# Graph layer kernel: edge codes spread by broadcasting DMA reads, weighted destination one-hots made by GpSimd alone

## The chip, the cores and the metric

The kernel runs on one core of a Trainium2 chip. The time is the device time of one execution in microseconds (us). The engines are named as the profile names them: PE is TensorE (matmuls), PEld its weight loads, DVE is VectorE, ACT is ScalarE, POOL is GpSimd, SP is SyncE, which here only issues DMAs (SPq is its queue). Each runs its own list of instructions in order; between engines the order is held by semaphores (`wait_ge` and `then_inc`).

## What is computed

```python
# x: 1250 x 512; src, dst: 41250 edges, sorted by dst before the kernel sees them
h = relu(layernorm(x))
m = relu(concat(h[src], h[dst]) @ W0.T + b0)           # one message per edge
x = x + segment_sum(m, src)                            # "S" in the kernel
h = relu(layernorm(x))
g = (h @ W1.T)[src] * edge_weight
out = segment_sum(g, dst)
x = x + where(out >= 0, out, alpha * out)
```

The kernel splits the first product in two (A = h Wa for sources, B = h Wb + b for destinations), so a message is relu(A[src] + B[dst]). The second layer becomes a matrix: M[src, dst] is the sum of the weights of the edges from src to dst, and the result is M.T (h W1.T).

## The kernel before

Nodes stand in 10 blocks of 125. Stage one (to about 339 us) sorts the edges into tiles of 128 that have one source block and one destination block each, puts for each tile the local source number (`local_s`), the local destination number (`local_d`) and the weight (as a high and a low part, `weight_h`, `weight_l`) of each edge on the partitions, and computes A and B, each as a high and a low part. Stage two is the edge loop (to about 1053 us), which the change is in. Stage three is the second layer (to the end).

The edge loop goes over 108 groups (`NGRP`) of 4 tiles (`GRP`); the tiles of a group make two pairs (`PAIR`), called h = 0 and h = 1 here. For group g:

- ACT needs the codes of the edges along the free dimension and on all 125 partitions. `row_d` and `row_s` hold them as one row for each group. PE spreads a row over the partitions by a matmul with a column of the identity (`spread`, L881, into the PSUM tile `spread_ps`), ACT squares the difference to the partition's own number (`square_of`, L990) and turns it into a one-hot (`one_hot_of`, L995: `turned_d`, `turned_s`).
- PE makes a message tile j by four matmuls (L931, L932 with `turned_d`; L936, L937 with `turned_s`) into `edge_ps[j]`. ACT takes the relu and its high part (`msg_hi`, L1014), DVE the low part (`msg_lo`, L1086). PE sums the messages over the sources with two matmuls (`sum_tile`, L886, with the one-hot `hot_s`), DVE adds them to S (`add_sums`, L1059).
- For M, DVE makes one-hots of the destinations (`make_hots(hot_d, ...)`, L1097) and POOL multiplies them with the two parts of the weights (`weigh`, L838, into `hot_w[h]`). PE multiplies them with the one-hots of the sources (`weights`, L896, two matmuls into `m_ps`). ACT copies the result out (`copy_weights`, L1000, into `pair_w[h]`), DVE adds the parts (`join_weights`, L1069), and POOL adds the two 125 x 125 squares to M (`add_weights`, L850). I write W(g, h) for the two matmuls of `weights(g, ..., h)`.

The order around the change is written out by hand:

- PE in group g (L919): tile 0, spread of the destinations of g + 1, sums of tile 2 of g - 1; tile 1, spread of the sources of g + 1, sums of tile 3 of g - 1, W(g - 1, 0); tile 2, sums of tile 0; tile 3, then (L914) sums of tile 1 and W(g - 1, 1).
- DVE in group g (L1081): msg_lo of tile 0; of tile 1, S of g - 1, join of (g - 2, 1); msg_lo of tile 2, `hot_d` of g + 1; msg_lo of tile 3, `hot_s` of g + 1 (L1103, after W(g - 1, 1)), S of g, join of (g - 1, 0).
- POOL in group g (L864): weigh (g, 0), add (g - 1, 0), weigh (g, 1), add (g - 1, 1). `weigh` waits for the matmuls that last read the buffer (L844), `add_weights` for the join (L853). One buffer `hot_w[h]` stands for each h.
- PE waits in `weights(g, ..., h)` for both parts of `hot_w[h]` of g:

```python
pe.wait_ge(hots_w, g * 4 + 2 * h + 2)
```

Of the kernel before, what the change touches and what calls it, by code (L numbers as in the profile page):

```python
# [20 lines left out]
ALU = mybir.AluOpType  # L21
# [9 lines left out]
P = 128  # L31
# [9 lines left out]
GRP = 4  # L41
PAIR = 2
# [34 lines left out]
def build(nc, x, src, dst, edge_weight, w0, b0, w1, alpha, out):  # L77
    table_dram = nc.dram_tensor("edge_table", [P * NT, TABLE_FIELDS], F32).ap()
    with ExitStack() as top:
# [25 lines left out]
        expand_at = sb("expand_at", [1, NGRP, 2 * GRP], I32)  # L105
        gather_at = sb("gather_at", [1, NGRP, 2 * GRP], I32)

# [31 lines left out]
        with ExitStack() as scope:  # L139
            def sb1(name, shape, dt, where=scope):  # L140
                return sb(name, shape, dt, where)


# [115 lines left out]
            with nc.Block() as block:  # L259
# [28 lines left out]
                def _(pool):  # L288
# [70 lines left out]
                    own(pool.tensor_copy(weight_h[:], weight_all))  # L359
                    pool.tensor_tensor(weight_l[:], weight_all, weight_h[:].bitcast(F32), ALU.subtract)  # L360

                @block.vector
                def _(dve):
# [191 lines left out]
                    own(dve.tensor_scalar(local_d[:], code[:].bitcast(I32), 1.0 / 65536.0, None, ALU.mult))  # L555
                    own(dve.tensor_scalar(local_s[:], local_d[:], -(TILE - 1) / 2, 1.0 / TILE, ALU.add, ALU.mult))
                    own(dve.tensor_scalar(local_s[:], local_s[:], MAGIC, None, ALU.add))
                    own(dve.tensor_scalar(local_s[:], local_s[:], -MAGIC, None, ALU.add))
                    own(dve.scalar_tensor_tensor(out=local_d[:], in0=local_s[:], scalar=-float(TILE), in1=local_d[:],
# [229 lines left out]
        hot_d = [sb(f"hot_d{k}", [P, GRP, OHW], BF16, scope) for k in range(2)]  # L789
# [5 lines left out]
        row_s = sb("row_s", [NGRP, GRP * P], BF16, scope)  # L795
        row_d = sb("row_d", [NGRP, GRP * P], BF16, scope)
# [8 lines left out]
        spread_ps = psum_scope.enter_context(nc.psum_tensor("spread_ps", [BN, GRP * P], F32))  # L805
# [4 lines left out]
        hots_d = sem("hots_d")  # L810
# [3 lines left out]
        spread_ready = sem("spread_ready")  # L814
# [12 lines left out]
        with nc.Block() as block:  # L827
            @block.gpsimd
            def _(pool):
# [39 lines left out]
                weigh(0, 0, 0, first=True)  # L869
                weigh(0, 0, 1, first=True)  # L870
# [9 lines left out]
            def _(pe):  # L880
                def spread(row, g):  # L881

                    pe.matmul(spread_ps[:], ident_b[0:NGRP, bass.ds(g, 1)].to_broadcast([NGRP, BN]), row[:],  # L883
                              start=True, stop=True).then_inc(spread_ready, 1)

# [33 lines left out]
                def group(g, k, at, first=False, second=False, last=False, load_next=False, whole=True):  # L919
# [3 lines left out]
                    for j in range(GRP):  # L923
# [42 lines left out]
                pe.wait_ge(rows_out, 1)  # L966
                spread(row_d, 0)
                pe.wait_ge(rows_out, 2)
                pe.wait_ge(squared, 1)
                spread(row_s, 0)  # L970
# [18 lines left out]
            def _(act):  # L989
                def square_of(n):  # L990

                    act.wait_ge(spread_ready, n)
                    act.activation(square[:], spread_ps[:], ACT.Square, bias=minus_no[0:BN, :]).then_inc(squared, 1)  # L993
# [14 lines left out]
                def group(g, k, start=None, last=False):  # L1008

                    for j in range(GRP):  # L1010
# [5 lines left out]
                        if j == 0 and not last:  # L1016
                            act.wait_ge(turned, g * 2 + 2)
                            square_of(g * 2 + 3)
                        if j == 0 and start not in (0, 1):
                            copy_weights(g - 2, 1, first=start == 2)  # L1020
                        if j == 1 and not last:
                            one_hot_of(g * 2 + 3, turned_d[1 - k])
                            act.wait_ge(turned, g * 2 + 3)
                            square_of(g * 2 + 4)
# [8 lines left out]
                square_of(1)  # L1033
                one_hot_of(1, turned_d[0])
                act.wait_ge(turned, 1)
                square_of(2)
                one_hot_of(2, turned_s[0])
                for g in range(UNROLL + 2):
                    group(g, g % 2, start=g)
                with act.Fori(1, (NGRP - 4) // UNROLL) as it:  # L1040
                    for i in range(UNROLL):
                        group(it * UNROLL + 2 + i, i % 2)
                group(NGRP - 2, 0)
# [341 lines left out]
```

## Time and profile before

| | |
|---|---|
| median of 3 runs | 1177.44 us (1175.58 to 1181.98) |
| the profiled execution | 1174.35 us, its span from first to last instruction 1172.7 us |
| PE busy | 1077.3 us (92%) |
| DVE, ACT, POOL busy | 974.6 us (83%), 815.8 us (70%), 716.2 us (61%) |
| granted TensorE clock, mean | 0.964 |
| edge loop | about 339 to 1053 us |

The profile is one execution. Busy time is summed over all stages, so its shares say little of one stage; for the edge loop the order of single instructions in time says most. A matmul's recorded end is a model, and its record is longer than the time until the next may start, so for PE starts are compared with starts.

### The profile page before, as it was taken

The numbers are of one execution on the slowest core, as the hardware profiler recorded it, in microseconds if no ns is written. First come the engines' busy times: TensorE is split into PE (matmuls) and PEld (weight loads), VectorE is DVE, ScalarE is ACT, GpSimd is POOL, SyncE is SP. The second block draws the span as 40 slices with busy tenths as digits, with TensorE's granted clock in tenths as the row PEclk, the third lists the DMA queues.
The fourth block names the chain that finished last, engine by engine and source line by source line (L and its number), as shares of the span: only waits on it lengthen the run. The fifth ranks groups of instructions, "written<-read, shape, count | busy, mean of one in ns | idle before, by whom it ended". The sixth has DMA issues, their size and how long they took to land. (4 is left out here: it accounts for less than half of the span.)

```text
span 1172.7 us, 22759 instructions
## 1 busy us (share of the span) xinstructions
PE 1077.3 (92%) x5106; PEld 846.5 (72%) x5107; DVE 974.6 (83%) x1810; ACT 815.8 (70%) x1660; POOL 716.2 (61%) x1043
## 2 busy tenths in 40 slices
PE   2388989898989999999999999999999999978997
PEld 2156767566658888888888888888888888857776
DVE  7667888888748999999999999999999999975453
ACT  3555656566758888888888888888888888855210
POOL 5482858585845767776777777777777776660000
PEclk9659999999989999999999999999999999988999
DMA  4000000000000000000000000000000000000011
GB/s 170 23 3 1 3 2 3 2 3 2 2 16 1 0 0 0 0 0 0 0 0 0 0 0 0 0 0 0 0 0 0 0 0 0 0 6 31 10 35 44
DMA packets 8988, 10.48 MB, mean 9 GB/s; under 512 B 4699, under 2 KB 5174, under 8 KB 8955
## 3 DMA queue, kind: packets, MB, share of 16 engines
q1 hardware_dynamic: 4635, 9.78, 2.5%
q0 software_dynamic: 4320, 0.29, 1.4%
q8 instruction: 17, 0.28, 0.1%
q14 instruction: 16, 0.13, 0.0%
HBM read 6.65 MB, written 3.14 MB: 8 GB/s over the span
## 5 line engine op out<-in xcount | busy, mean ns | idle before, releaser
L862 POOL TENSOR_TENSOR M<-M,pair_w 125x125 f32 x432 | 219.8, 509 | 200.2 <-DVE pair_w L1072 160.7
L1086 DVE SCALAR_TENSOR_TENSOR msg_lo<-edge_ps,msg_hi 128x512 fp32r<-128x512 f32 x432 | 294.4, 687 | 55.4 <-ACT msg_hi L1014 50.4
L1014 ACT ACTIVATE msg_hi<-edge_ps 128x512 fp32r<-128x512 f32 x432 | 258.8, 599 | 104.5 <-PE edge_ps L937 104.4
L354 POOL DMA_INDIRECT edge_table<-fields,row_no x135 | 179.1, 1326 | 92.8 <-DVE row_no L420 50.9
L892 PE MATMUL node_ps<-msg_hi,hot_s 128*125 128x512 f32 x432 | 212.0, 491 | 0.2 <-DVE msg_lo L1086 0.2
L597 PE MATMUL psum<-hot_tile,lane_piece 125*128 125x432 f32 x585 | 159.6, 398 | 40.1 <-ACT lane_piece L704 37.0
L704 ACT ACTIVATE lane_piece<-hot_lane,fields 125x128 fp32r<-125x128 bf16 x390 | 126.0, 391 | 77.5 <-DVE hot_lane L432 71.6
L931 PE MATMUL edge_ps<-b_hi,turned_d 125*128 x432 | 172.7, 400 | 0.7 <-issue 0.7
L936 PE MATMUL edge_ps<-a_hi,turned_s 125*128 x432 | 171.0, 396 | 0.0
L932 PE MATMUL edge_ps<-b_lo,turned_d 125*128 x432 | 170.9, 396 | 0.0
L893 PE MATMUL node_ps<-msg_lo,hot_s 128*125 128x512 f32 x432 | 170.2, 394 | 0.0
L937 PE MATMUL edge_ps<-a_lo,turned_s 125*128 x432 | 170.1, 394 | 0.0
L846 POOL TENSOR_TENSOR hot_w<-hot_d,weight_l 128x252 fp32r<-128x252 bf16 x216 | 167.1, 774 | 0.0
L597 PEld LDWEIGHTS psum<-hot_tile,lane_piece 125*128 125x128 f32 x585 | 104.9, 196 | 73.1 <-ACT lane_piece L704 40.7
L993 ACT ACTIVATE square<-spread_ps,minus_no 125x512 f32<-125x512 f32 x216 | 148.1, 686 | 11.5 <-PE spread_ps L883 0.2
L1067 DVE TENSOR_TENSOR S<-S,node_ps 125x512 f32 x216 | 147.5, 683 | 2.4
L846 POOL TENSOR_TENSOR hot_w<-hot_d,weight_h 128x252 fp32r<-128x252 bf16 x216 | 131.4, 608 | 5.4 <-DVE hot_d L1077 3.4
L1006 ACT COPY pair_w<-m_ps 125x504 f32<-125x504 f32 x216 | 124.9, 578 | 4.1 <-POOL M L862 4.0
L430 DVE TENSOR_SCALAR hot_tile<-iota,tile_no 125x432 fp32r<-125x432 f32 x195 | 98.1, 503 | 30.2 <-PE psum L597 29.5
L1072 DVE TENSOR_TENSOR pair_w<-pair_w 125x252 f32<-125x252 f32 x216 | 106.8, 494 | 2.5 <-ACT pair_w L1006 2.5
L892 PEld LDWEIGHTS node_ps<-msg_hi,hot_s 128*125 128x125 f32 x432 | 80.5, 186 | 26.9 <-DVE msg_lo L1086 0.7
L903 PEld LDWEIGHTS m_ps<-hot_w,hot_s 128*125 128x125 f32 x432 | 80.3, 186 | 23.1 <-POOL hot_w L846 2.6
(213 smaller groups left out, 1858.9 us busy)
## 6 DMA issues: line engine op xcount, KB each, us to landing
S<-in_x_dram SPq DMA_DIRECT2D x1, 2500.0 KB
out_dram<-result SPq DMA_DIRECT2D x10, 250.0 KB
edge_table<-fields,row_no POOLq DMA_INDIRECT x135
w_in<-in_L_gnn_W_dram SPq DMA_DIRECT2D x1, 2048.0 KB, 11.6
w_in<-in_L_gnn_W_dram SPq DMA_DIRECT2D x1, 1024.0 KB, 5.3
edge_table<-zeros SPq DMA_DIRECT2D x1, 432.0 KB, 31.8
raw<-edge_table SPq DMA_DIRECT2D x1, 432.0 KB, 2.9
src_i<-in_src_dram SPq DMA_DIRECT2D x1, 161.1 KB
```

What stands on the lines that cost most here:

```text
L354: pool.indirect_dma_start(table_dram[:, :], bass.IndirectOffsetOnAxis(ap=row_no[:, c:c + 1], axis=0), fields[:, c, 0:TABLE_FIELDS], None). ...
L597: mm = pe.matmul(code_ps if f == 0 else weight_ps, lane_piece[r][:, f, :], hot_tile[r][:], start=(q == 0 and f < 2), stop=True, skip_group ...
L846: pool.tensor_tensor(hot_w[h][:, :, f, :], hot_d[k][:, h * PAIR:(h + 1) * PAIR, :], part[:, bass.ds(g * GRP + h * PAIR, PAIR)].unsqueeze(2 ...
L862: pool.tensor_tensor(part, part, pair_w[h][:, j, 0, 0:BN], ALU.add).then_inc(m_added, 1)
L892: pe.matmul(sums[:], hot_s[k][:, j, 0:BN], msg_hi[j][:], start=(j % PAIR == 0), stop=False)
L893: pe.matmul(sums[:], hot_s[k][:, j, 0:BN], msg_lo[j][:], start=False, stop=(j % PAIR == PAIR - 1)).then_inc(tile_summed, 1)
L931: pe.matmul(edge_ps[j][:], td, b_hi[:, b_rows], start=True, stop=False)
L932: pe.matmul(edge_ps[j][:], td, b_lo[:, b_rows], start=False, stop=False)
L936: pe.matmul(edge_ps[j][:], ts, a_hi[:, a_rows], start=False, stop=False)
L937: pe.matmul(edge_ps[j][:], ts, a_lo[:, a_rows], start=False, stop=True).then_inc(edge_ready, 1)
L1014: act.activation(msg_hi[j][:], edge_ps[j][:], ACT.Relu).then_inc(hi_ready, 1)
L1086: dve.scalar_tensor_tensor(out=msg_lo[j][:], in0=edge_ps[j][:], scalar=0.0, in1=msg_hi[j][:].bitcast(F32), op0=ALU.max, op1=ALU.subtract). ...
```

## The change

Two things are changed in the edge loop. First, the rows of codes are written to DRAM once, and SP reads one row for each group and kind back with a DMA that repeats it over 125 partitions (`spread`, four buffers, two for each kind); ACT squares from these buffers, and the spread matmuls and `spread_ps` are gone. Second, DVE no longer makes `hot_d`. POOL copies the three numbers of each edge of the group (destination, two weight parts) into a small tile (`take_edges`) and makes each weighted one-hot with one compare-and-multiply instruction for each tile and part: 8 instructions of 126 columns for each group in the place of 4 of 252. POOL's order in a group becomes: add (g - 1, 0), weigh (g, 0), add (g - 1, 1), weigh (g, 1), and `weigh` has no wait of its own. The four arrays `local_d`, `weight_h`, `weight_l` become one, `edge`, in which the three numbers of an edge stand together. PE's order is the same apart from the spreads, and DVE's apart from `hot_d`.

```diff
+    rows_dram = nc.dram_tensor("edge_rows", [2, NGRP, GRP * P], BF16).ap()
...
-        local_d = sb("local_d", [P, NT], F32)
-        weight_h = sb("weight_h", [P, NT], F32R)
-        weight_l = sb("weight_l", [P, NT], F32)
+        edge = sb("edge", [P, NT, 3], F32)
+        local_d, weight_h, weight_l = (edge[:, :, f] for f in range(3))
...
-        hot_d = [sb(f"hot_d{k}", [P, GRP, OHW], BF16, scope) for k in range(2)]
+        edge_of = [sb(f"edge_of{k}", [P, GRP, 3], F32, scope) for k in range(2)]
...
+            @block.sync
+            def _(sp):
+                for f, row in enumerate((row_d, row_s)):
+                    sp.wait_ge(rows_out, f + 1)
+                    sp.dma_start(rows_dram[f], row[:]).then_inc(rows_stored[f], 16)
+                for g in range(NGRP):
+                    for f in range(2):
+                        k = g % SPREADS * 2 + f
+                        if g == 0:
+                            sp.wait_ge(rows_stored[f], 16)
+                        if g >= SPREADS:
+                            sp.wait_ge(squared, (g - SPREADS) * 2 + f + 1)
+                        sp.dma_start(spread[k][:], rows_dram[f, g:g + 1, :].to_broadcast([BN, GRP * P])).then_inc(spread_in[k], 16)
...
-                def weigh(g, k, h, first=False):
-                    if h == 0:
-                        pool.wait_ge(hots_d, g + 1)
-                    if not first:
-                        pool.wait_ge(m_ready, g * 2 + h - 1)
-                    for f, part in enumerate((weight_h[:].bitcast(F32), weight_l)):
-                        pool.tensor_tensor(hot_w[h][:, :, f, :], hot_d[k][:, h * PAIR:(h + 1) * PAIR, :],
-                                           part[:, bass.ds(g * GRP + h * PAIR, PAIR)].unsqueeze(2)
-                                           .to_broadcast([P, PAIR, OHW]), ALU.mult).then_inc(hots_w, 1)
+                def take_edges(g, k):
+                    pool.tensor_copy(edge_of[k][:], edge[:, bass.ds(g * GRP, GRP), :]).then_inc(edges_taken, 1)
+
+                def weigh(k, h):
+                    for f in range(2):
+                        for j in range(PAIR):
+                            at = h * PAIR + j
+                            ins = pool.tensor_scalar(hot_w[h][:, j, f, :], iota[:, 1:1 + OHW], edge_of[k][:, at, 0:1],
+                                                     edge_of[k][:, at, 1 + f:2 + f], ALU.is_equal, ALU.mult)
+                        ins.then_inc(hots_w, 1)
...
                 def group(g, k, second=False):
+                    take_edges(g, k)
+                    pool.wait_ge(edges_taken, g + 1)
                     for h in range(2):
-                        weigh(g, k, h)
                         add_weights(g - 1, h, first=second)
+                        weigh(k, h)
...
-                        if j == 0 and not last:
-                            pe.wait_ge(squared, g * 2 + 2)
-                            spread(row_d, g + 1)
-                        if j == 1 and not last:
-                            pe.wait_ge(squared, g * 2 + 3)
-                            spread(row_s, g + 1)
...
-                def square_of(n):
-                    act.wait_ge(spread_ready, n)
-                    act.activation(square[:], spread_ps[:], ACT.Square, bias=minus_no[0:BN, :]).then_inc(squared, 1)
+                def square_of(k, f, turn):
+                    act.wait_ge(spread_in[k * 2 + f], turn * 16 + 16)
+                    act.activation(square[:], spread[k * 2 + f][:], ACT.Square, bias=minus_no[0:BN, :]).then_inc(squared, 1)
...
-                        if j == 2 and not last:
-                            if start != 0:
-                                dve.wait_ge(hots_w, g * 4)
-                            make_hots(hot_d[1 - k], local_d, g + 1).then_inc(hots_d, 1)
```

## Rows read from the trace of the kernel before

**Rows 1.** The page, part 1: busy time of each engine, share, instructions.

```profile
PE 1077.3 (92%) x5106; PEld 846.5 (72%) x5107; DVE 974.6 (83%) x1810; ACT 815.8 (70%) x1660; POOL 716.2 (61%) x1043
```

**Rows 2.** Windows: stretch, length, busy PE, PEld, DVE, ACT, POOL, clock, DMA share, GB/s.

```profile
354.37:1041.65 687.28, 687.12 (x3179) 554.66 (x3178) 639.49 (x1059) 576.52 (x1060) 489.71 (x843) 1.00 0.00 0
162.00:168.00 6.00, 3.56 (x16) 2.25 (x15) 6.00 (x17) 3.31 (x11) 0.00 (x0) 1.00 0.00 0
...
342.00:348.00 6.00, 5.11 (x12) 3.21 (x12) 0.69 (x1) 3.36 (x7) 6.00 (x2) 0.50 0.00 0
```

**Rows 3.** Timeline of the start of the loop: first square, first W.

```profile
341.53 0.69 ACT L993 ACTIVATE square<-spread_ps,minus_no 125x512 f32<-125x512 f32 x1
...
354.37 0.39 PE L903 MATMUL m_ps<-hot_w,hot_s 128*125 128x252 f32 x2
```

**Rows 4.** Timeline of the end of the loop: W(106, 0), last W, last add.

```profile
1041.65 0.39 PE L903 MATMUL m_ps<-hot_w,hot_s 128*125 128x252 f32 x2
...
1049.13 0.78 PE L903 MATMUL m_ps<-hot_w,hot_s 128*125 128x252 f32 x2 [2.37 <-POOL hot_w L846]
...
1052.54 0.40 POOL L862 TENSOR_TENSOR M<-M,pair_w 125x125 f32 x1 [0.17 <-POOL M L862]
```

**Rows 5.** Timeline of PE over one group: start, length in us, engine, line.

```profile
403.93 0.38 PE L883 MATMUL spread_ps<-row_d,ident_b 108*125 108x512 bf16 x1
...
406.23 0.39 PE L903 MATMUL m_ps<-hot_w,hot_s 128*125 128x252 f32 x2
...
408.57 0.39 PE L937 MATMUL edge_ps<-a_lo,turned_s 125*128 x1
...
409.27 0.40 PE L903 MATMUL m_ps<-hot_w,hot_s 128*125 128x252 f32 x2
...
412.73 0.39 PE L903 MATMUL m_ps<-hot_w,hot_s 128*125 128x252 f32 x2
```

**Rows 6.** Waits of the engines, 420 to 1000 us: us in total, times, longest.

```profile
POOL M L862 <- DVE pair_w L1072: 130.6, 176, 1.7
```

**Rows 7.** Timeline of ACT, DVE and POOL behind the same group.

```profile
409.08 0.60 ACT L1014 ACTIVATE msg_hi<-edge_ps 128x512 fp32r<-128x512 f32 x1
...
409.71 0.69 DVE L1086 SCALAR_TENSOR_TENSOR msg_lo<-edge_ps,msg_hi 128x512 fp32r<-128x512 f32 x1 [0.21 <-ACT msg_hi L1014]
...
410.30 0.60 POOL L846 TENSOR_TENSOR hot_w<-hot_d,weight_l 128x252 fp32r<-128x252 bf16 x1
410.32 1.12 DVE L1077 TENSOR_TENSOR hot_s<-iota,local_s 128x504 fp32r<-128x504 f32 x1
...
411.96 0.41 DVE L1072 TENSOR_TENSOR pair_w<-pair_w 125x252 f32<-125x252 f32 x1
...
412.56 0.45 POOL L862 TENSOR_TENSOR M<-M,pair_w 125x125 f32 x1 [1.65 <-DVE pair_w L1072]
...
413.19 0.46 POOL L862 TENSOR_TENSOR M<-M,pair_w 125x125 f32 x1 [0.18 <-PE m_ps L903]
...
413.60 0.61 POOL L846 TENSOR_TENSOR hot_w<-hot_d,weight_h 128x252 fp32r<-128x252 bf16 x1
```

**Rows 8.** Timeline of DVE where no POOL instruction stands beside it.

```profile
358.46 0.67 DVE L1077 TENSOR_TENSOR hot_s<-iota,local_s 128x504 fp32r<-128x504 f32 x1
...
359.05 0.68 DVE L1067 TENSOR_TENSOR S<-S,node_ps 125x512 f32 x1
...
359.64 0.41 DVE L1072 TENSOR_TENSOR pair_w<-pair_w 125x252 f32<-125x252 f32 x1
```

**Rows 9.** Lines by form, POOL, stage one: busy us, mean ns, idle before.

```profile
L318 POOL TENSOR_SCALAR local<-local 125x330 f32<-125x330 f32 x1 | 0.5, 509 | 0.1
...
L338 POOL TENSOR_SCALAR bkt_small<-bkt_small 100x1 f32<-100x1 f32 x1 | 0.2, 192 | 0.1
```

**Rows 10.** DMA issues of the page: name, size, us from issue to landing.

```profile
raw<-edge_table SPq DMA_DIRECT2D x1, 432.0 KB, 2.9
```

**Rows 11.** Waits of SP's queue: us in total, times, longest.

```profile
SPq L1185 <- DMA out_dram<-result: 3.7, 1, 3.7
```

More of the change, by code:

```diff
@@ L554, in _ @@
                     own(dve.tensor_tensor(code[:], raw[:, :, CODE_AT], code_ps, ALU.add))
-                    own(dve.tensor_scalar(local_d[:], code[:].bitcast(I32), 1.0 / 65536.0, None, ALU.mult))
-                    own(dve.tensor_scalar(local_s[:], local_d[:], -(TILE - 1) / 2, 1.0 / TILE, ALU.add, ALU.mult))
+                    own(dve.tensor_scalar(local_d, code[:].bitcast(I32), 1.0 / 65536.0, None, ALU.mult))
+                    own(dve.tensor_scalar(local_s[:], local_d, -(TILE - 1) / 2, 1.0 / TILE, ALU.add, ALU.mult))
                     own(dve.tensor_scalar(local_s[:], local_s[:], MAGIC, None, ALU.add))
                     own(dve.tensor_scalar(local_s[:], local_s[:], -MAGIC, None, ALU.add))
-                    own(dve.scalar_tensor_tensor(out=local_d[:], in0=local_s[:], scalar=-float(TILE), in1=local_d[:],
+                    own(dve.scalar_tensor_tensor(out=local_d, in0=local_s[:], scalar=-float(TILE), in1=local_d,
                                                  op0=ALU.mult, op1=ALU.add))
@@ L788, in build @@
         hot_s = [sb(f"hot_s{k}", [P, GRP, OHW], F32R, scope) for k in range(2)]
-        hot_d = [sb(f"hot_d{k}", [P, GRP, OHW], BF16, scope) for k in range(2)]
+        edge_of = [sb(f"edge_of{k}", [P, GRP, 3], F32, scope) for k in range(2)]
         hot_w = [sb(f"hot_w{h}", [P, PAIR, 2, OHW], F32R, scope) for h in range(2)]
         pair_w = [sb(f"pair_w{h}", [BN, PAIR, 2, OHW], F32, scope) for h in range(2)]
-        row_s = sb("row_s", [NGRP, GRP * P], BF16, scope)
-        row_d = sb("row_d", [NGRP, GRP * P], BF16, scope)
+        spread = [sb(f"spread{k}", [BN, GRP * P], BF16, scope) for k in range(2)]
+        with ExitStack() as rows:
+            row_s = sb("row_s", [NGRP, GRP * P], BF16, rows)
+            row_d = sb("row_d", [NGRP, GRP * P], BF16, rows)
+        spread += [sb(f"spread{k}", [BN, GRP * P], BF16, scope) for k in range(2, 2 * SPREADS)]
         square = sb("square", [BN, GRP * P], F32, scope)
@@ L813, in build @@
         hots_w = sem("hots_w")
-        spread_ready = sem("spread_ready")
+        rows_stored = [sem(f"rows_stored{f}") for f in range(2)]
+        spread_in = [sem(f"spread_in{k}") for k in range(2 * SPREADS)]
         squared = sem("squared")
@@ L864, in group @@
                 def group(g, k, second=False):
+                    take_edges(g, k)
+                    pool.wait_ge(edges_taken, g + 1)
                     for h in range(2):
-                        weigh(g, k, h)
                         add_weights(g - 1, h, first=second)
-                weigh(0, 0, 0, first=True)
-                weigh(0, 0, 1, first=True)
+                        weigh(k, h)
+                take_edges(0, 0)
+                pool.wait_ge(edges_taken, 1)
+                weigh(0, 0)
+                weigh(0, 1)
                 pool.memset(M[:], 0.0).then_inc(m_clear, 1)
@@ L1006, in copy_weights, with group @@
                     act.copy(pair_w[h][:], m_ps[:]).then_inc(m_copied, 1)
-                def group(g, k, start=None, last=False):
+                def group(g, k, turn, start=None, last=False):
                     for j in range(GRP):
@@ L1032, in _ @@
                     act.copy(row[:], edge_ps[f][0:NGRP, :]).then_inc(rows_out, 1)
-                square_of(1)
+                square_of(0, 0, 0)
                 one_hot_of(1, turned_d[0])
                 act.wait_ge(turned, 1)
-                square_of(2)
+                square_of(0, 1, 0)
                 one_hot_of(2, turned_s[0])
                 for g in range(UNROLL + 2):
-                    group(g, g % 2, start=g)
+                    group(g, g % 2, (g + 1) // 2, start=g)
                 with act.Fori(1, (NGRP - 4) // UNROLL) as it:
                     for i in range(UNROLL):
-                        group(it * UNROLL + 2 + i, i % 2)
-                group(NGRP - 2, 0)
-                group(NGRP - 1, 1, last=True)
+                        group(it * UNROLL + 2 + i, i % 2, it * (UNROLL // 2) + (3 + i) // 2)
+                group(NGRP - 2, 0, (NGRP - 1) // 2)
+                group(NGRP - 1, 1, None, last=True)
                 copy_weights(NGRP - 2, 1)
```

25 lines of the change are left out of this document (9 added, 16 removed).

## Prediction

> **What bounds the kernel now.** I began with the shares of busy time: PE leads with 92%, DVE follows with 83% [rows 1]. Shares over all stages don't say what a change in the edge loop is worth, so next came the table of stretches for the loop alone. From the first W to W(106, 0) it takes 687.28 us, and PE is busy in 687.12 of them at a granted clock of 1.00, the full 2.4 GHz [rows 2]. PE has no gap there. Between the two stand 106 groups [rows 3, 4]: (1041.65 - 354.37) / 106 = 6.484 us a group. One group is 16 message matmuls, 8 sums, two W (two matmuls of 252 columns each, together one slot of 512) and two spreads, 28 slots of 6.484 / 28 = 0.2316 us. The single group says the same: W(g - 1, 0) starts at 406.23 and W(g, 0) at 412.73 [rows 5]. So PE bounds the loop, and 24 + 2 = 26 slots, 6.02 us, would be left without spreads.
>
> The next question is what is late once PE is faster. I followed, in the timeline, who waits for whom around W, as the change reorders POOL there. Now POOL weighs group g first and then waits for the join of g - 1; 130.6 us of its time from 420 to 1000 us are that wait [rows 6]. It costs nothing, as `hot_w` of g is already made: its two parts are done by 410.90, and W(g, 0) reads it at 412.73 [rows 5, 7].
>
> **The change: the new cycle.** Now weigh(g, 0) stands behind add(g - 1, 0) on POOL. That add waits for DVE's join of (g - 1, 0), which waits for ACT's copy of W(g - 1, 0), and stands on DVE behind `msg_lo` of the last tile, `hot_s` and S. W(g, 0) waits for the weigh. So from W(g - 1, 0) to W(g, 0) there is a closed chain, and a group can't be shorter than it. In the old trace the join ended at 412.37 and POOL's first add began at 412.56, while PE read the buffer at 412.73 [rows 5, 7]: two adds and a whole weigh too late. I walk the chain with W(g - 1, 0) = 406.23 as zero:
>
> - PE: 10 matmuls until L937 of tile 3 starts, 408.57, +2.34 [rows 5]. No spread stands between, so this stays.
> - ACT: msg_hi of tile 3 at 409.08, +2.85 [rows 7].
> - DVE: msg_lo at 409.71, +3.48; it waited for ACT, so it gains nothing from the missing `hot_d`. `hot_s` at 410.32, +4.09 [rows 7]. It also waits for W(g - 1, 1), which stands 3.04 behind W(g - 1, 0) [rows 5], so that is met.
> - `hot_s` takes 1.12 us here, beside POOL's multiply from 410.30 [rows 7]. In the new order POOL has nothing to weigh at that point (it finished weigh(g - 1, 1) about 2 us after zero and waits for this join), so I take the undisturbed spacing: S starts 0.59 after `hot_s`, the join 0.59 after S, and lasts 0.41 [rows 8]. Join ends at 4.09 + 0.59 + 0.59 + 0.41 = +5.68.
> - POOL: first add 0.19 later (412.37 to 412.56), second 0.63 later, the next instruction 0.41 later [rows 7]: +5.87, +6.50, +6.91.
> - POOL: four compare-and-multiply instructions of step s; then W. PE's first matmul after such a wait is longer by a weight load that nothing hides: W(107, 1) took 0.78 for the usual 0.39 [rows 4, 5]. I take 0.05 for the signal and 0.20 of that. Cycle = 6.91 + 4s + 0.25 = 7.16 + 4s.
>
> **The step s.** The trace has no such instruction of 126 columns with operands read for each partition. The nearest are POOL's two-operation scalar instructions: 192 ns with 1 column, 509 ns with 330 [rows 9], hence 192 + 317 x 125 / 329 = 312 ns with 126. From below, one column's 0.19 a step. From above, the two-input multiply of 252 columns, 0.60 [rows 7]. I take s = 0.30, nearest to the first pair, as the successor on POOL starts a little before the recorded end and the per-partition operands may add a little. Cycle = 7.16 + 1.20 = 8.36 us; bounds 7.92 and 9.56.
>
> The Trainium skill, GPSIMD Engine Reference, Performance pitfalls for Q7 kernels, says that a body that compares costs twice the time per element unless it is unrolled by two. No run here shows it; it speaks against this change, and it is the third case below.
>
> The Trainium skill, SBUF — State Buffer, Who interferes with whom, says that a DVE instruction with two SBUF inputs and a GpSimd instruction that reads SBUF shut each other out. By that rule, the trace agrees (1.12 against 0.67 for `hot_s`), the new instructions still block `hot_s` if they meet; then 0.45 would come on top of the cycle, 8.81. By the timeline above they don't meet.
>
> **The other parts.** PE loses 2 slots a group, 0.46 us, and it has slack afterwards: 6.02 of work in 8.36, so this gain is gone (49 us if PE still bounded). DVE loses `hot_d`, off the chain. The h = 1 chain is W(g - 1, 1), tiles 0 and 1 of g + 1, their msg_lo, S, join, add, weigh: by the same spacings about 7.6 us, shorter, so it adds no second stall. POOL's small copy falls into its wait for the join. ACT squares from SBUF instead of PSUM; ACT was idle for over 100 us of the 687 [rows 2] and is under no load in 8.36. SP's DMAs are issued two groups ahead, some 16 us, against landings of 2.9 and 3.7 us [rows 10, 11]; 125 KB each 4 us is little beside the 432 KB that landed in 2.9. If that cover went, ACT's squares would be late, which needs landings over 12 us.
>
> **Start and end.** The first square now comes after a store to DRAM and a read back: 3.7 and 2.9 us by the two rows, less for smaller sizes [rows 10, 11], in the place of a spread matmul. With the store issued somewhat before the first square of 341.53 [rows 3], that square moves to 346 to 348: I take +5 (bounds 3 and 8). At the end, W(107, 0), add(106, 1), weigh(107, 1), W(107, 1), copy, join, add follow each other; from W(106, 0) to the last add I count 12.7 us in place of 1052.94 - 1041.65 = 11.3 [rows 4]: +1.4.
>
> **Sum.** 106 x (8.36 - 6.484) = +198.9; + 5 + 1.4 = +205. The profiled execution took 1174.35, which gives 1379.6; it lies 3 below the median of the runs, so I say 1381. 0.5% of 1177 is about what a measurement of this kernel can tell from no change.
>
> **Rivals.**
>
> 1. The chain binds, s between 0.22 and 0.36: cycle 8.04 to 8.60, 1347 to 1406 us. For it: every wait in it is written in the code, and its pieces have rows. Chance 0.59.
> 2. PE still bounds, because the weigh is in time (I misread an order, or the engines run further ahead than the chain allows): faster than before. The price is 6.02 for 6.484, -49, and +6 at start and end: 1134 us. It decides where the cycle falls under 6.43; the join alone ended 5.68 behind W, so adds and weigh would have to fit into 0.5 us. Chance 0.06, of which 0.01 near no change.
> 3. The compare costs twice per element. A POOL instruction that moves 125 columns at the double rate is the add to M: 0.45 us [rows 7]. With s = 0.40 to 0.45, cycle 8.76 to 8.96, +241 to +263 with 6.4 at the ends: 1424 to 1445 us. Chance 0.17. With s of 0.60, or with `hot_s` blocked besides, 1500 and more. Chance 0.05.
> 4. PE's clock falls, since PE now stands 2.3 us of 8.4. Against it: from 162 to 168 us PE was busy only 3.56 of 6.00, 2.44 without a matmul, and the clock stayed at 1.00; at the loop's start, after PE had mostly stood, it was 0.50, that is 1.2 GHz [rows 2]. At that level the 26 slots take 12.0 us, more than the chain: 106 x (12.0 - 6.48) = +590 at worst; half of the groups cold gives about 1575. Chance 0.06.
> 5. The chain is shorter than I count (s near 0.20, hops cheaper): under 1347 us, still over 1300. Chance 0.07.
>
> The range of 8 in 10 goes from case 1's low end to case 3's: 1340 to 1450. Slower 0.94, same 0.01, faster 0.05.
>
> **What the changed profile should show.** W to W at 8.4 us; PE idle about 2.3 us once a group before L903 of h = 0, released by POOL's hot_w, and PE's busy share of the loop near 72%; POOL's first add waiting for the join, and a four-instruction weigh of about 1.2 us right behind the second; `hot_s` at 0.67, no longer 1.12; the clock at 1.00; no wait of ACT for the DMA after the start. I am wrong if the stall is at another place (ACT for spread_in, or DVE), if PE shows no stall, or if a POOL instruction takes over 0.4 us.

## The result and the profile after

The changed kernel takes 1766.49 us in the median (1763.45 to 1769.33, four runs), against 1179.68 for the kernel before on the same chip: a ratio of 1.498, interval 1.492 to 1.504. Forecast were 1381 us, 1340 to 1450. The sign was right and the price was about a third of the real one: +205 in place of +587.

The profiled execution took 1767.1 us. Its page, parts 1, 2 (clock row) and 5: busy time, granted clock in 40 slices, costliest groups (busy us, mean ns, idle before).

```profile
PE 1260.6 (71%) x4890; PEld 965.9 (55%) x4891; DVE 885.8 (50%) x1702; ACT 833.8 (47%) x1660; POOL 1083.1 (61%) x1583
...
PEclk8699999887777788778778777777877877877899
...
L870 POOL TENSOR_SCALAR hot_w<-iota,edge_of 128x126 fp32r<-128x126 f32 x864 | 674.7, 795 | 0.1
...
L887 POOL TENSOR_TENSOR M<-M,pair_w 125x125 f32 x432 | 184.3, 427 | 426.1 <-DVE pair_w L1083 389.6
L927 PE MATMUL m_ps<-hot_w,hot_s 128*125 128x252 f32 x432 | 127.3, 386 | 405.6 <-POOL hot_w L870 405.6
...
L1004 ACT ACTIVATE square<-spread,minus_no 125x512 f32<-125x512 bf16 x216 | 155.3, 719 | 8.3 <-DMA spread<-edge_rows 4.8
```

PE issues 216 instructions fewer than before and is "busy" for 183 us more [rows 1]. That is no more work: the clock row is full of 7 and 8, so the same matmuls take longer. PE stands 405.6 us for POOL's `hot_w`, POOL stands 389.6 us for DVE's join, and each new instruction takes 795 ns. ACT's squares wait for the DMAs 4.8 us in all.

The table of stretches, columns as in [rows 2], for the loop:

```profile
365.00:1625.00 1260.00, 864.97 (x2955) 668.66 (x2953) 549.18 (x952) 591.75 (x1055) 843.93 (x1368) 0.79 0.07 21
```

PE was busy without a pause at 1.00 before [rows 2]; now it is busy for 69% at 0.79. The timeline of one group follows; it answers to [rows 5, 7].

```profile
707.58 0.78 PE L927 MATMUL m_ps<-hot_w,hot_s 128*125 128x252 f32 x2 [3.88 <-POOL hot_w L870]
...
708.16 0.64 PE L955 MATMUL edge_ps<-b_hi,turned_d 125*128 x1
...
708.46 3.12 POOL L870 TENSOR_SCALAR hot_w<-iota,edge_of 128x126 fp32r<-128x126 f32 x4
708.59 0.63 PE L956 MATMUL edge_ps<-b_lo,turned_d 125*128 x1
...
712.00 0.63 PE L961 MATMUL edge_ps<-a_lo,turned_s 125*128 x1
...
713.04 0.39 PE L927 MATMUL m_ps<-hot_w,hot_s 128*125 128x252 f32 x2
...
713.30 0.69 DVE L1097 SCALAR_TENSOR_TENSOR msg_lo<-edge_ps,msg_hi 128x512 fp32r<-128x512 f32 x1 [1.87 <-ACT msg_hi L1025]
...
713.90 0.67 DVE L1088 TENSOR_TENSOR hot_s<-iota,local_s 128x504 fp32r<-128x504 f32 x1
...
715.09 0.42 DVE L1083 TENSOR_TENSOR pair_w<-pair_w 125x252 f32<-125x252 f32 x1
...
715.77 0.46 POOL L887 TENSOR_TENSOR M<-M,pair_w 125x125 f32 x1 [4.05 <-DVE pair_w L1083]
...
716.83 3.13 POOL L870 TENSOR_SCALAR hot_w<-iota,edge_of 128x126 fp32r<-128x126 f32 x4
...
720.01 0.79 PE L927 MATMUL m_ps<-hot_w,hot_s 128*125 128x252 f32 x2 [3.79 <-POOL hot_w L870]
```

From one W(g, 0) to the next (707.58 to 720.01) runs the closed chain of the prediction: ten matmuls, `msg_hi`, `msg_lo`, `hot_s`, S, join, two adds, four compares of 0.78 us. PE is cold behind its pause (0.63 us records, 0.43 apart), so the last matmul of tile 3 starts 4.42 behind W (712.00), where 2.34 were predicted. The formula at s = 0.78 gives 10.28, the cold matmuls add 2.08, and the group took 12.43 us. The four compares that begin at 708.46 are the weigh of h = 1; it is done before W(g, 1) needs it at 713.04.

In the table of waits from 380 to 1200 us (us in total, times, longest), about 69 groups, PE waits for `hot_w` 69 times, once a group, and DVE's `hot_s` has no row: it waits for nothing but DVE's own order.

```profile
PE m_ps L927 <- POOL hot_w L870: 258.9, 69, 3.9
```

The first W and W(106, 0) in the timeline, as in [rows 3, 4], with the first square and the last add:

```profile
348.85 0.72 ACT L1004 ACTIVATE square<-spread,minus_no 125x512 f32<-125x512 bf16 x1 [4.15 <-DMA spread<-edge_rows]
...
361.94 0.39 PE L927 MATMUL m_ps<-hot_w,hot_s 128*125 128x252 f32 x2
...
1627.61 0.78 PE L927 MATMUL m_ps<-hot_w,hot_s 128*125 128x252 f32 x2 [3.57 <-POOL hot_w L870]
...
1645.37 0.40 POOL L887 TENSOR_TENSOR M<-M,pair_w 125x125 f32 x1 [0.17 <-POOL M L887]
```

106 groups lie between the two W: (1627.61 - 361.94) / 106 = 11.94 us each, for 6.484 before. The loop thus lost 106 x 5.456 = 578.4 us; the start is 7.6 later, and the tail from W(106, 0) to the end of the last add is 18.2 for 11.3. Together 592.8, and the spans differ by 1765.4 - 1172.7 = 592.7. So 578 of the 593 us are in the period of the loop, and 14 at its two ends. In what follows the period of every kernel is read this way, first W to W(106, 0).

### The profile page after: what moved, and what is told of

It is laid out like the page before. It is cut to its first block and busy times, and to the rows that moved or that the text cites. A ratio compares the mean times of both kernels' runs of the same rounds, so it can differ in the third digit from the quotient of the medians.

```text
span 1765.4 us, 22439 instructions
## 1 busy us (share of the span) xinstructions
PE 1260.6 (71%) x4890; PEld 965.9 (55%) x4891; DVE 885.8 (50%) x1702; ACT 833.8 (47%) x1660; POOL 1083.1 (61%) x1583
## 5 line engine op out<-in xcount | busy, mean ns | idle before, releaser
L870 POOL TENSOR_SCALAR hot_w<-iota,edge_of 128x126 fp32r<-128x126 f32 x864 | 674.7, 795 | 0.1
L887 POOL TENSOR_TENSOR M<-M,pair_w 125x125 f32 x432 | 184.3, 427 | 426.1 <-DVE pair_w L1083 389.6
L927 PE MATMUL m_ps<-hot_w,hot_s 128*125 128x252 f32 x432 | 127.3, 386 | 405.6 <-POOL hot_w L870 405.6
L955 PE MATMUL edge_ps<-b_hi,turned_d 125*128 x432 | 210.2, 486 | 6.3 <-ACT turned_d L1009 6.3
L960 PE MATMUL edge_ps<-a_hi,turned_s 125*128 x432 | 208.4, 482 | 0.9 <-ACT turned_s L1009 0.9
L961 PE MATMUL edge_ps<-a_lo,turned_s 125*128 x432 | 208.1, 482 | 0.0
L956 PE MATMUL edge_ps<-b_lo,turned_d 125*128 x432 | 207.9, 481 | 0.0
L1004 ACT ACTIVATE square<-spread,minus_no 125x512 f32<-125x512 bf16 x216 | 155.3, 719 | 8.3 <-DMA spread<-edge_rows 4.8
L955 PEld LDWEIGHTS edge_ps<-b_hi,turned_d 125*128 125x128 f32 x432 | 112.1, 259 | 22.7 <-issue 6.7
L960 PEld LDWEIGHTS edge_ps<-a_hi,turned_s 125*128 125x128 f32 x432 | 104.3, 241 | 28.8 <-issue 1.6
```

What stands on the lines that cost most here:

```text
L870: ins = pool.tensor_scalar(hot_w[h][:, j, f, :], iota[:, 1:1 + OHW], edge_of[k][:, at, 0:1], edge_of[k][:, at, 1 + f:2 + f], ALU.is_equal, ...
L887: pool.tensor_tensor(part, part, pair_w[h][:, j, 0, 0:BN], ALU.add).then_inc(m_added, 1)
L927: mm = pe.matmul(m_ps[:, j], hot_s[k][:, h * PAIR + j, 0:BN], hot_w[h][:, j], start=True, stop=True)
L955: pe.matmul(edge_ps[j][:], td, b_hi[:, b_rows], start=True, stop=False)
L956: pe.matmul(edge_ps[j][:], td, b_lo[:, b_rows], start=False, stop=False)
L960: pe.matmul(edge_ps[j][:], ts, a_hi[:, a_rows], start=False, stop=False)
```

## Experiments

Three suspects stood for the missing 382 us: the price of the new instruction, a further chain, and the clock.

**1. The price of the instruction by itself.** The kernel before, with POOL, which has nothing to do in stage three, running each form three times there.

```diff
+ pool.tensor_scalar(pb_r[...], iota[:, 1:127], edge_no, edge_w, ALU.is_equal, ALU.mult)   # L1184
+ pool.tensor_scalar(pb_r[...], iota[:, 1:127], 5.0, 0.5, ALU.is_equal, ALU.mult)          # L1186
+ pool.tensor_scalar(pb_r[...], iota[:, 1:253], edge_no, edge_w, ALU.is_equal, ALU.mult)   # L1188
...
+ pool.tensor_scalar(pb_r[...], iota[:, 1:127], edge_no, edge_w, ALU.mult, ALU.mult)       # L1196
+ pool.tensor_scalar(pb_r[...], iota[:, 1:127], 5.0, 0.5, ALU.mult, ALU.mult)              # L1200
```

> The kernel before, with ten small series of GpSimd instructions added in stage three, where POOL has nothing to do; they write to a tile that nobody reads. In the changed kernel the compare-and-multiply of 126 columns takes 0.78 us a step. Theory A, the price is a fixed one of the two operands that are read for each partition: with constants the same instruction takes about 0.30 us, with 252 columns and per-partition operands about 0.9, with 32 columns about 0.7. Theory B, the price is per column (the compare): 252 columns take 1.4 to 1.5 us, 32 columns 0.25 to 0.35, and a multiply-multiply of 126 columns with per-partition operands takes 0.3 to 0.4. The kernel's time should stay within 1% of 1180 us by both.

Lines by form, POOL, in that stretch (busy us, mean ns of one):

```profile
L1188 POOL TENSOR_SCALAR pb_r<-iota,local_d,weight_l 128x252 fp32r<-128x252 f32 x3 | 3.6, 1208 | 0.1
...
L1184 POOL TENSOR_SCALAR pb_r<-iota,local_d,weight_l 128x126 fp32r<-128x126 f32 x3 | 2.4, 804 | 0.4 <-POOLq L827 0.4
...
L1186 POOL TENSOR_SCALAR pb_r<-iota 128x126 fp32r<-128x126 f32 x3 | 1.9, 641 | 0.2
...
L1196 POOL TENSOR_SCALAR pb_r<-iota,local_d,weight_l 128x126 fp32r<-128x126 f32 x3 | 1.3, 443 | 0.0
...
L1200 POOL TENSOR_SCALAR pb_r<-iota 128x126 fp32r<-128x126 f32 x3 | 0.9, 301 | 0.2
```

The time was 1178.09 us, as without the series. Neither theory is right alone: the price is by column (1208 ns for 252 columns, 471 for 32), and the operands add a smaller part that is the same for 126 and 252 columns (163 ns, and 1208 - 1054 with constants = 154). Two multiplies by constants take 301 ns; [rows 9] had given me 312, so the interpolation was right for the instruction that it described. The compare in the place of one multiply adds 340 (641 - 301), and the operands read for each partition add 163 (804 - 641; 142 without the compare, 443 - 301). From 126 to 252 columns the new instruction grows by 404, or 3.2 ns a column, where [rows 9] grew by 0.96. The Trainium skill, GPSIMD Engine Reference, Performance pitfalls for Q7 kernels, puts a body that compares, if it isn't unrolled by two, at twice the time per element; the sign agrees, and here it is over three times.

**2. The order alone.** The kernel before with POOL's add ahead of its weigh; spreads, `hot_d` and multiplies stay.

```diff
                     for h in range(2):
-                        weigh(g, k, h)
                         add_weights(g - 1, h, first=second)
+                        weigh(g, k, h)
```

> The kernel before with one change: POOL adds group g - 1 before it weighs group g. Spreads by matmul, hot_d by DVE and the two-input multiplies (0.57 us a step) stay. Theory A, the chain from W(g - 1, 0) to W(g, 0) binds: 6.91 + 2 x 0.57 + 0.04 + 0.25 = 8.34 us a group for 6.484, +197 us, 1377 us, with PE standing 1.9 us once a group and the clock at 1.00. Rival, the order costs nothing and all of the loss is the slow instruction on POOL: 1180 us. Third, any regular standing of PE lowers the clock: a clock under 0.95 in the loop and 1450 us or more.

1369.44 us, ratio 1.162 (1.156 to 1.169), 8.25 us a group. The timeline of PE's W(g, 0) and of what leads to the next:

```profile
699.97 0.50 PE L903 MATMUL m_ps<-hot_w,hot_s 128*125 128x252 f32 x2 [1.55 <-POOL hot_w L846]
...
704.16 0.67 DVE L1077 TENSOR_TENSOR hot_s<-iota,local_s 128x504 fp32r<-128x504 f32 x1
705.35 0.41 DVE L1072 TENSOR_TENSOR pair_w<-pair_w 125x252 f32<-125x252 f32 x1
...
706.01 0.46 POOL L862 TENSOR_TENSOR M<-M,pair_w 125x125 f32 x1 [3.42 <-DVE pair_w L1072]
...
707.06 0.60 POOL L846 TENSOR_TENSOR hot_w<-hot_d,weight_h 128x252 fp32r<-128x252 bf16 x1
...
708.28 0.49 PE L903 MATMUL m_ps<-hot_w,hot_s 128*125 128x252 f32 x2 [1.54 <-POOL hot_w L846]
```

`hot_s` stands at +4.19 (predicted +4.09), the join at +5.38 (5.27), the first add at +6.04 (5.87), the weigh at +7.09 (6.91), the next W at +8.31. The chain, walked in the old trace, is right to 0.2 us at every step, and the order alone costs 190 us. The third theory fails: PE stands once in each group, and the clock of the loop is 1.00 (table of stretches).

```profile
380.00:1200.00 820.00, 672.06 (x2985) 513.44 (x2984) 585.07 (x995) 547.06 (x995) 394.78 (x794) 1.00 0.00 0
```

**3. The spreads by DMA alone.** The kernel before with the rows stored, the broadcasting reads and the `edge` array, and no spread matmul; order and multiplies as before.

> The changed kernel with the DMA reads of the rows only: hot_d by DVE, the two-input multiplies and the old order on POOL are back. Theory A, PE bounds with 26 slots: 6.02 us a group, -49 us and +7.5 at the start (the first W came 7.5 us later in the changed kernel): 1138 us. Rival, DVE is next, as its busy time is 6.03 us a group with collisions: 6.1 to 6.3 us a group, 1147 to 1168 us. Third, the DMA reads themselves hold ACT up: 1180 us or more, with a wait of ACT for the spread buffers.

1164.7 us, ratio 0.988 (0.982 to 0.994), 6.29 us a group, not 6.02. PE in the loop is busy all the time by the records, as the late matmul hides in the length of the one before it. The timeline shows what W waits for:

```profile
705.17 0.57 ACT L1012 COPY pair_w<-m_ps 125x504 f32<-125x504 f32 x1
...
705.50 0.40 PE L912 MATMUL node_ps<-msg_lo,hot_s 128*125 128x512 f32 x1
...
705.88 0.47 PE L922 MATMUL m_ps<-hot_w,hot_s 128*125 128x252 f32 x2
```

W(g, 0) starts 0.38 behind the matmul before it, not 0.23, and the matmul behind W comes 0.31 later instead of 0.23: both h share one PSUM tile `m_ps`, and ACT's copy of the last W ends at 705.74. The time lies in the range of the rival, in which DVE binds; experiment 8 decides between the two.

**4. All of the change with PE kept busy.** Fourteen matmuls a group more, ahead of W(g, 0), into a PSUM bank that nobody reads.

```diff
                         if j == 1 and not first:
+                            for _ in range(14):
+                                pe.matmul(idle_ps[:], hot_s[1 - k][:, 3, 0:BN], msg_hi[3][:], start=True, stop=True)
                             weights(g - 1, 1 - k, 0, first=second)
```

> The changed kernel with 14 matmuls of 512 columns put before W(g, 0) on PE, into a PSUM tile that nobody reads. In the changed kernel PE stands about 4 us there, so at 2.4 GHz they (3.2 us) fit into the stall. Theory A, the clock falls because PE stands: now it stays near 1.00, the group takes 7.16 + 4 x 0.78 = 10.3 us, and the kernel 1175 + 8 + 106 x (10.28 - 6.484) = 1585 to 1600 us, faster than the changed kernel by about 170 in spite of more work. Rival, the clock has nothing to do with it and the 11.8 us a group are all chain: 1766 us as before or, as the fillers delay W, up to 1850.

1672.28 us, ratio 1.421 (1.414 to 1.429): with more work on PE the kernel is 94 us faster. The table of stretches for its loop:

```profile
365.00:1520.00 1155.00, 1039.58 (x4396) 770.08 (x4395) 559.24 (x943) 574.80 (x1044) 857.30 (x1363) 1.00 0.07 23
```

The clock is 1.00, and the period 11.02, not the 7.16 + 4 x 0.78 = 10.28 of the prediction's formula. The timeline shows why:

```profile
702.01 0.49 PE L928 MATMUL m_ps<-hot_w,hot_s 128*125 128x252 f32 x2 [0.75 <-POOL hot_w L871]
...
702.66 0.68 DVE L1091 TENSOR_TENSOR hot_s<-iota,local_s 128x504 fp32r<-128x504 f32 x1 [0.43 <-PE m_ps L928]
...
704.60 0.41 POOL L888 TENSOR_TENSOR M<-M,pair_w 125x125 f32 x1 [2.50 <-DVE pair_w L1086]
...
705.56 3.23 POOL L871 TENSOR_SCALAR hot_w<-iota,edge_of 128x126 fp32r<-128x126 f32 x4
...
709.82 3.13 POOL L871 TENSOR_SCALAR hot_w<-iota,edge_of 128x126 fp32r<-128x126 f32 x4
...
713.08 0.49 PE L928 MATMUL m_ps<-hot_w,hot_s 128*125 128x252 f32 x2 [0.93 <-POOL hot_w L871]
```

The waits from 380 to 1200 us have a row that the changed kernel's don't have, once in each of the 75 groups:

```profile
DVE hot_s L1091 <- PE m_ps L928: 37.8, 75, 0.6
```

Here a second closed chain binds. W(g, 1) is late, `hot_s` waits for it, then come S, the join of h = 0, two adds, the weigh of h = 0, two adds, the weigh of h = 1, and W(g + 1, 1). It holds both weighs of a group. The mean period less eight compares, 11.02 - 8 x 0.78 = 4.78, is its rest. So the period is the larger of 7.16 + 4s and 4.78 + 8s, which cross at s = 0.60.

**5. The DMA spreads and the order, without compares.** The kernel of experiment 3 with the add ahead of the weigh.

> The changed kernel with hot_d by DVE and the two-input multiplies of before, but with the DMA reads and with the new order on POOL. It differs from the kernel with the order alone (1369 us) only in who spreads the rows. Theory A, the chain from W to W binds and PE's two slots less are worth nothing: 8.3 us a group, 1369 + 7.5 at the start = 1377 us. Rival, PE's slots count here too: 0.46 x 106 = 49 us less, 1328 us.

1471.67 us, ratio 1.245 (1.237 to 1.253): neither of the two. Experiment 3 gained 15 us and experiment 2 lost 190, and both together lose 292. The timeline of PE:

```profile
702.08 0.49 PE L922 MATMUL m_ps<-hot_w,hot_s 128*125 128x252 f32 x2 [1.71 <-POOL hot_w L869]
702.41 0.39 PE L950 MATMUL edge_ps<-b_hi,turned_d 125*128 x1
...
710.42 0.63 PE L922 MATMUL m_ps<-hot_w,hot_s 128*125 128x252 f32 x2 [2.00 <-POOL hot_w L869]
```

The table of stretches for its loop:

```profile
380.00:1200.00 820.00, 660.06 (x2502) 503.43 (x2503) 523.19 (x894) 497.67 (x895) 356.84 (x719) 0.88 0.09 28
```

One group runs warm in 8.34 us, the chain of experiment 2. After the pause of 2.00 the next starts cold. The distance from W(g, 0) to W(g, 1) tells the two kinds apart in the timeline, about 3.1 us warm and mostly 4.7 cold. Of 100 groups, 4 to 103, 67 start cold, behind pauses of 1.73 to 2.06, and 33 warm, behind pauses of 1.37 to 1.99; in experiment 2 all pauses of these groups are 1.38 to 1.59, and all start warm. The mean period is 9.15.

**6. Half of the compares.** The change with only the high part of the weights made (M lacks the low parts), so two instructions for each h.

```diff
-                    for f in range(2):
+                    for f in range(1):
                         for j in range(PAIR):
...
-                        ins.then_inc(hots_w, 1)
+                        ins.then_inc(hots_w, 2)
```

> The changed kernel without the low part of the weights: POOL makes 4 compare-and-multiply instructions a group in the place of 8, the other half of each buffer stays zero, so M lacks the low parts. Two chains can bind: W(g - 1, 0) to W(g, 0), 7.16 + n x 0.78 with n instructions in a weigh, and the one through both weighs, 4.77 + 2n x 0.78 (from the kernel with the busy PE: 11.01 with n = 4). With n = 2 they are 8.72 and 7.89. Theory A, the first binds and the clock stays at 1.00 (PE stands 2.7 us): 1175 + 8 + 106 x (8.72 - 6.484) = 1420 us. Theory B, the clock falls as in the changed kernel: plus up to 1.5 us a group, 1500 to 1580 us. Theory C, POOL's busy time binds by itself: its load of 3.12 + 2.1 + 0.2 us is no bound at all, so a time near 1180 us would show the order harmless.

1552.51 us, ratio 1.317 (1.313 to 1.321), 9.95 us a group, for 8.72 by the first chain: theory B. PE's pauses are about 2.2 us, and the loop's granted clock is 0.84.

**7. POOL's old order with the compares.** The change with the weigh ahead of the add again. The copy of the edge's numbers is split in two, one ahead of each weigh, and it carries the wait for the matmuls that last read `hot_w[h]`; the register load for the adds stands behind it.

> The changed kernel with POOL's old order: it weighs (g, h) before it adds (g - 1, h), and waits for the matmuls that last read the buffer. Its 8 slow instructions stay. Theory A, POOL's own work now binds: 8 x 0.78 + 2 x 1.04 for the adds + 2 x 0.35 for the small copies = 9.0 us a group, 1175 + 8 + 106 x (9.02 - 6.484) = 1452 us if PE's clock stays, up to 1500 if it falls at times. Rival, the chains bind in this order too: 1600 us or more.

1617.45 us, ratio 1.372 (1.368 to 1.376), 10.50 us a group: the number of the rival. Leaving the order as it was saves only 149 of 587. POOL's timeline:

```profile
702.23 3.13 POOL L873 TENSOR_SCALAR hot_w<-iota,edge_of 128x126 fp32r<-128x126 f32 x4 [0.77 <-POOL edge_of L864]
...
705.95 0.45 POOL L889 TENSOR_TENSOR M<-M,pair_w 125x125 f32 x1 [0.17 <-POOL M L889]
706.34 0.64 POOL L864 COPY edge_of<-edge 128x6 f32 x1
707.75 3.13 POOL L873 TENSOR_SCALAR hot_w<-iota,edge_of 128x126 fp32r<-128x126 f32 x4 [0.77 <-POOL edge_of L864]
```

POOL has no gap but 0.17 between the two adds and 0.77 behind each small copy, where the program has the wait for the copy and the register load for the adds. So POOL may be the bound itself, as in theory A, whose 9.0 us lacked twice 0.77; experiment 12 tests it.

**8. A kernel faster than both.** Experiment 3 with a PSUM bank for each h, so W(g, 0) needs no copy of W(g - 1, 1).

```diff
-        m_ps = psum_scope.enter_context(nc.psum_tensor("m_ps", [BN, PAIR, 2, OHW], F32))
+        m_ps = psum_scope.enter_context(nc.psum_tensor("m_ps", [BN, 2, D], F32))
...
-                        pe.wait_ge(m_copied, g * 2 + h)
+                        pe.wait_ge(m_copied, g * 2 + (1 if h else -1))
```

> The kernel with the DMA reads alone (1165 us), with the PSUM bank that the spreads left used for a second m_ps, so that W(g, 0) needn't wait for ACT's copy of W(g - 1, 1). In the former kernel that copy ended at 705.74 and W began at 705.88, some 0.2 us late. Theory A, this wait is what keeps the group at 6.28 us and not at 6.02: 6.05 to 6.1 us a group, 1141 to 1147 us. Rival, DVE binds (5.97 us of busy time a group): 1160 to 1168 us.

1149.33 us, ratio 0.974 (0.971 to 0.977), 6.15 us a group, a little over theory A's 6.05 to 6.1 and under the rival's times. So the wait for the copy was about half of what kept experiment 3 above 6.02, and DVE wasn't its bound. This is the best kernel here; what the 0.13 above 26 slots is wasn't tried.

**9 and 10. Is it the clock in experiment 5, and what would keep it?** Its kernel with eight and with two matmuls a group more ahead of W(g, 0), written as in experiment 4. Two is what the DMA spreads took off PE.

> The kernel of the experiment before (spreads by DMA, one-hots multiplied by POOL with its add ahead of its weigh) with eight matmuls more a group ahead of W(g,0), into a PSUM bank that nobody reads; they wait for nothing and fit within the 2.0 us for which TensorE stood idle there (8 x 0.2316 = 1.85 us). Theory, the clock: that kernel took 1471.7 only because TensorE was granted 0.88 in the loop; kept busy it is granted 1.00, W(g,0) follows POOL's hot_w every 8.3 us as in the kernel with the order alone (1369.4), and the time is 1370 to 1385, although TensorE has more to do. Rival, the missing 100 us lie elsewhere (the broadcasting reads, DVE's later hot_d): the time stays at 1465 or more, with a granted clock of 1.00 or without it.

> The same with two matmuls more a group instead of eight: just the number that the DMA spreads took off TensorE, so it issues 28 a group again and stands idle for about 1.5 us in 8.3, as in the kernel with the order alone (idle 1.55 us, clock 1.00, 1369.4). Theory, what matters is how much TensorE does between its pauses: clock 1.00 and 1370 to 1385, so the two matmuls that the change takes off TensorE cost some 90 us by their absence. Rival, the fall of the clock in that kernel comes from where its pauses lie and not from their length: clock still 0.88 to 0.95 and 1430 to 1470.

1373.65 us (ratio 1.165, 1.162 to 1.168) and 1370.35 us (1.162, 1.160 to 1.165). The loop of the kernel with two, in the table of stretches:

```profile
380.00:1200.00 820.00, 675.09 (x2975) 520.47 (x2974) 584.42 (x993) 546.20 (x993) 395.83 (x796) 1.00 0.10 31
```

Two W(g, 0) of it in PE's timeline:

```profile
704.00 0.50 PE L923 MATMUL m_ps<-hot_w,hot_s 128*125 128x252 f32 x2 [1.50 <-POOL hot_w L870]
...
712.16 0.50 PE L923 MATMUL m_ps<-hot_w,hot_s 128*125 128x252 f32 x2 [1.36 <-POOL hot_w L870]
```

Two matmuls whose result nobody reads make the kernel of experiment 5 faster by 101 us. The clock is 1.00, the period 8.26, that of the order alone (8.25). All pauses of groups 4 to 103 are 1.34 to 1.55, and no group starts cold. The missing 100 us of experiment 5 were the clock: with it restored nothing is left for the broadcasting reads or another cause. That the two matmuls shorten the pause and that they raise PE's work between pauses comes together here; which of the two keeps the clock wasn't separated.

**11. Half of the compares with PE kept busy** (nine more matmuls a group in the kernel of experiment 6), the test of the whole model.

> The kernel with half of the compares (the low parts of the weights left out, so M misses them) with nine matmuls more a group ahead of W(g,0), into a PSUM bank that nobody reads, so that TensorE's pauses of 2.2 us are filled. Theory, two chains at full clock: with two instructions for each h the first chain is 7.16 + 2 x 0.78 = 8.72 us a group and the second 4.77 + 4 x 0.78 = 7.89, so the first binds: 1179.7 + 7.5 + 1.4 + 106 x (8.72 - 6.484) = 1426 us, 1415 to 1435, clock 1.00. The 126 us to the kernel without fillers (1552.5) are then the clock. Rival: it stays over 1480, another chain that I don't count.

1426.49 us, ratio 1.213 (1.210 to 1.215), clock 1.00, 8.76 us a group for 8.72. The 0.04 would be 5 us; that the totals agree to 0.5 is luck. Here the clock had cost 126.

**12. The old order with the compares and PE kept busy** (seven more matmuls ahead of each W in the kernel of experiment 7).

> The kernel with POOL's old order (weigh ahead of add) and all eight compares, with seven matmuls more ahead of each W, into a PSUM bank that nobody reads. Theory: there POOL itself is the bound, with nothing between its instructions but the register load behind the small copy (4 x 0.78 + two adds of 0.6 + copy 0.2 to 0.6 + 0.77 idle, twice a group, 10.5 to 11); its clock of 0.86 costs nothing, so with TensorE busy at 1.00 the time stays at 1600 to 1625 us (1617.4 without). Rival, a chain through TensorE binds there too: the time falls by over 30 us, to under 1590.

1613.58 us, ratio 1.370 (1.368 to 1.373), 10.48 us a group. The table of stretches for its loop:

```profile
380.00:1200.00 820.00, 776.91 (x3287) 575.87 (x3286) 421.15 (x704) 429.21 (x780) 672.36 (x1093) 1.00 0.07 24
```

A full clock instead of 0.86 moves it by 4 us. POOL bounds it: its 672.36 us of work and 0.77 idle twice in each of the 820 / 10.48 = 78 groups (120) make 793 of 820, and the 0.17 between the two adds, twice a group, is the other 27. The text above puts the 0.77 down to the register load; the trace shows only the idle time.

## Why the prediction failed

The time in steps, as the runs have it:

| kernel | us | period | clock in the loop |
|---|---|---|---|
| before | 1180 | 6.48 | 1.00 |
| order alone (2) | 1369 | 8.25 | 1.00 |
| order, DMA spreads, PE filled (10) | 1370 | 8.26 | 1.00 |
| and compares, PE filled (4) | 1672 | 11.02 | 1.00 |
| after | 1766 | 11.94 | 0.79 |

- **What bounds the kernel, and the chain: right.** The steps of the walk came true to 0.2 us (experiment 2), the formula gave 8.72 us a group for a kernel with 8.76 (11), PE waits at W(g, 0) for POOL's `hot_w`, POOL waits for the join, `hot_s` runs at 0.67 undisturbed, and no square waits for a DMA in the loop.
- **The step s: mis-sized, the first failure.** 0.30 taken, 0.19 to 0.60 as bounds, 0.78 measured. The row behind 0.30 was of an instruction that multiplies by a constant and adds one, and both things in which the new one differs have a price: the compare 0.34, the operands 0.16. I knew of both and called one of them "a little". As the upper bound I took another instruction because it was long, though nothing made it an upper bound. In the formula s stands four times: 4 x 0.48 x 106 = 204 us.
- **The clock, the second failure: the rival with 0.06 came true beside the first.** The forecast had the clock at 1.00, and it was 0.79. In the changed kernel the cold matmuls stand in the first chain: it would be 10.28 a group at s = 0.78, and the period is 11.94, 1.66 x 106 = 176 us more. So the period's miss of 11.94 - 8.36 is 204 by s and 176 by the clock. A full clock gives back only 94 of the 176 (1766 to 1672), since then the second chain takes over at 11.02. My evidence against a fall was one stretch of 6 us in stage one with PE busy for 3.56 at 1.00 [rows 2]. That stretch is the same in the new kernel (busy 3.93, clock 1.00) and says nothing of a loop that pauses in each group: pauses up to 1.59 us in 8.3 left the clock at 1.00 (2, 10), pauses up to 2.06 did not (5).
- **"So it adds no second stall" and, of `hot_s` waiting for W(g - 1, 1), "that is met": wrong at the real s and a full clock.** I sized the h = 1 chain with one weigh in it. The chain that binds in experiment 4 holds two, since W(g, 1) feeds `hot_s` and so the join of h = 0. At s = 0.30 it is 4.78 + 2.40 = 7.18 and doesn't matter, at 0.78 it adds 11.02 - 10.28 = 0.74 a group, 78 us. In the changed kernel itself it doesn't bind, as the slowed first chain is longer: no W(g, 1) waits for POOL there, and no `hot_s` for W(g, 1). The terms of s and of this chain come to 282 of the 302 us between experiments 10 and 4; another 11 are the 0.10 a group by which the chain with multiplies was shorter than 8.36, 4 lie in the tail, and the rest is within the spread of the runs. The formula of the first chain was tested at a second size (11). That of the second rests on its timeline and one size.
- **"This gain is gone": too kind.** I priced the 2 slots that PE lost at nothing. Under a chain of 8.3 us they are a loss of 101 us (5 against 10), through the clock. Alone they gain 15 (3), 30 with a second PSUM bank (8).
- **The start: open.** The first W is 7.6 us later, where I said 5. From the issue of the store at 343.88 to the first square at 348.85 lie 5.0. But the first W of the other kernels stands anywhere from 356.2 to 367.3, at 361.5 in experiment 2, whose start is that of before. So the profile of one execution can't tell the route over DRAM from a late stage one. **The end**: 18.2 for 11.3, +6.9 instead of +1.4. The last W follow each other through weighs of 3.1 us.
- **Which cause is larger** has no single answer, as they don't add. The compares with the old order cost 434 (12), the order with multiplies 190 (2), both 493 (4); all but the second have the DMA spreads besides. With either one left in, most of the loss stays.

The range failed with s: its upper end let s reach 0.45, and the case of 0.60 and more had 0.05. With s of 0.78 put into my own formula it would have been 1174.35 + 106 x 3.80 + 6.4 = 1583 us.

## What to carry to other kernels

Before an order is changed, close the loop: find every chain that returns to the same instruction one period later, count how often the uncertain duration stands in it, and give the range that factor. An instruction that no row shows is priced by what it does to each element and by where its operands come from, and a longer row of another kind isn't its upper bound. Where a chain through TensorE and another engine becomes the bottleneck, TensorE's pauses can have a price of their own (94, 101 and 126 us here, none in experiment 2, and 4 where POOL's own work bound), and taking work off TensorE may then cost time; a few matmuls without use are a cheap way to find out. What a cause costs in the kernel and what its removal gives back can differ: the slow clock cost 176 us, and curing it gave 94, as the next chain stood close behind.

## What the runs showed of the chip

- POOL's compare-and-multiply of 128 x 126 with per-partition operands takes 804 ns, 1208 with 252 columns, 471 with 32; a single compare with one such operand 595 (experiment 1).
- The granted clock falls in a loop that pauses once a group for no more than about 2 us: pauses of 1.37 to 2.06 us, clock 0.88 (5); 1.34 to 1.59, clock 1.00 (2, 10). The Trainium skill, TensorE: Matmul & The Clock Gate, A second HAM failure mode: psum-queue depth-cycling, tells of short pauses between groups of matmuls that make the clock swing between its two levels. By that rule, the trace agrees in the swing: in experiment 5 one group shows records of 0.39 us, the next begins with 0.63. The pauses have another cause here, the wait for POOL's `hot_w`, where the page has the cycling through PSUM banks.
- POOL stands 0.77 us between a small copy that it waits for, with a register load behind it, and the next instruction (7, 12). What share the wait has in it and what share the load wasn't tried.
